# Exact search of a doubtful head rewrites its scores and threshold; one copy of the masking products

## The reference

```python
scores = jnp.einsum('bhqd,bhkd->bhqk', qn, kn)
temp = jax.nn.sigmoid(x.mean(axis=1) @ Wt + bt) + 0.5
scores = scores / temp[:, None, None, :]
kk = max(1, S // 4)
vals, idx = jax.lax.top_k(scores, kk)
w = jax.nn.softmax(vals, axis=-1)
rows = jnp.arange(B * H * S)[:, None]
attn = jnp.zeros((B * H * S, S), scores.dtype).at[rows, idx.reshape(-1, kk)].set(w.reshape(-1, kk)).reshape(B, H, S, S)
out = jnp.einsum('bhqk,bhkd->bhqd', attn, v)
```

## Time and profile before

| | us |
|---|---|
| median of three runs (3546.75 to 3565.47) | 3558.0 |
| the profiled execution | 3552.69 |
| its span, first to last instruction | 3550.8 |
| TensorE busy in it | 2939.5 |
| VectorE busy | 2754.0 |
| ScalarE busy | 2140.6 |
| GpSimd busy | 1797.6 |

### The profile page before, as it was taken

One profiled execution on the slowest core, in us unless ns is written; L12 is line 12 of the kernel. 1 busy time (PEld: TensorE's weight loads), 2 busy tenths in 40 slices (PEclk: granted clock), 3 DMA queues, 4 the chain that ended last, 5 costly groups with the idle time before them and its releaser, 6 DMA issues. The chain is left out here.

```text
span 3550.8 us, 59586 instructions
## 1 busy us (share of the span) xinstructions
PE 2939.5 (83%) x16154; PEld 1615.6 (45%) x16154; DVE 2754.0 (78%) x9472; ACT 2140.6 (60%) x5970; POOL 1797.6 (51%) x2285
## 2 busy tenths in 40 slices
PE   6798988878898689797887889788988889879755
PEld 3344444444454345454444445444544444444433
DVE  3787877878787787887878778787878888778872
ACT  2666666656666456665655667566665666566541
POOL 4355545545544455454554455465544556446533
PEclk9899999989998899999999999999989999899977
DMA  5000000000000000000000000000000000000000
GB/s 204 7 16 22 22 23 19 23 4 23 22 22 19 4 22 22 22 20 4 23 22 22 20 22 5 22 23 22 22 20 5 23 22 23 22 19 16 4 16 12
DMA packets 43575, 80.46 MB, mean 23 GB/s; under 512 B 3786, under 2 KB 11978, under 8 KB 43058
## 3 DMA queue, kind: packets, MB, share of 16 engines
q1 hardware_dynamic: 41554, 69.18, 5.8%
q0 software_dynamic: 1504, 5.77, 0.5%
HBM read 58.16 MB, written 16.78 MB: 21 GB/s over the span
## 5 line engine op out<-in xcount | busy, mean ns | idle before, releaser
L517 POOL TENSOR_SCALAR probs<-probs,kept_inv 128x256 f32<-128x256 f32 x1024 | 528.7, 536 | 892.1 <-DVE kept_inv L1769 892.1
L1730 DVE SCALAR_TENSOR_TENSOR probs<-scores,threshold,probs 128x256 f32<-128x256 f32 x1006 | 432.4, 493 | 206.9 <-issue 134.7
L1029 PE MATMUL work_ps<-ident,probs 128*128 128x128 f32 x2072 | 333.0, 297 | 182.9 <-POOL probs L517 123.6
L807 ACT ACTIVATE probsT<-work_ps 128x512 f32<-128x512 f32 x512 | 294.4, 596 | 303.8 <-PE work_ps L1029 287.9
L772 ACT ACTIVATE scores<-score_ps,neg_guess 128x256 f32<-128x256 f32 x1024 | 397.1, 483 | 103.7 <-DVE kept_inv L1769 98.1
L792 ACT ACTIVATE near<-scores 128x256 f32<-128x256 f32 x1024 | 412.8, 421 | 24.3 <-DVE nearest L1698 22.5
L1694 DVE MATCH_REPLACE8 near<-nearest,near 128x256 f32<-128x256 f32 x1024 | 406.9, 407 | 0.0
L1690 DVE MAX8 nearest<-near 128x8 f32<-128x256 f32 x1024 | 358.3, 411 | 6.3 <-DVE near L1682 4.7
L1029 PEld LDWEIGHTS work_ps<-ident,probs 128*128 128x128 f32 x2072 | 241.6, 149 | 263.2 <-POOL probs L517 120.2
L1698 DVE MAX8 nearest<-near 128x8 f32<-128x256 f32 x1024 | 356.9, 409 | 0.0
L484 POOL TENSOR_TENSOR inv_norm<-sumsq,minus_half 128x32 f32<-128x32 f32 x64 | 351.3, 5490 | 5.3
(11 more groups left out here) (171 smaller groups left out, 5535.4 us busy)
## 6 DMA issues: line engine op xcount, KB each, us to landing
x_in<-in_x_dram SPq DMA_DIRECT2D x32, 512.0 KB, 3.9
x_res<-in_x_dram SPq DMA_DIRECT2D x32, 512.0 KB, 4.6
out_dram<-rows SPq DMA_DIRECT2D x32, 512.0 KB, 3.1
c_sb<-in_ctx_dram SPq DMA_DIRECT2D x32, 256.0 KB, 2.7
scores<-in_L_ffn_W_dram SPq DMA_DIRECT2D x6, 1024.0 KB, 6.8
near<-in_L_ffn_W_dram SPq DMA_DIRECT2D x2, 1024.0 KB, 10.0
w_q<-in_L_attn_Wq_dram POOLq DMA_DIRECT2D x1, 1024.0 KB, 8.1
w_k<-in_L_attn_Wk_dram POOLq DMA_DIRECT2D x1, 1024.0 KB, 10.0
```

Source lines behind the costliest of these rows:

```text
L517: pool.tensor_scalar(probs[:, s % 2, h, j], probs[:, s % 2, h, j], kept_inv[:, s % 2, n:n + 1], 1.0, ALU.mult, ALU.mult).then_inc(s_pr, 1)
L807: act.activation(probsT[:, h, 2 * a:2 * a + 2], W[BANK_TP[s][2 * h + a]][:].rearrange("p (h k n) -> p h k n", h=2, k=NT), ACT.Copy).then_i ...
L1029: last = pe.transpose(dst[:, n * P:n * P + P], part, ident[:])
L1730: step.mark(dve.scalar_tensor_tensor(out=probs[:, r, h, j], in0=scores[:, r, h, j], scalar=threshold[:, r, k:k + 1], in1=probs[:, r, h, j] ...
```

## The change

A doubtful head's branch no longer ends in a product of its own. After the search, its scores are rewritten in place (1 where a score was struck out, else 0), its threshold is set to 0.5, and both are waited for. After the branches, eight `keep_above` stand once, and serve clean and doubtful units alike. The `Else` parts are gone, that of the unit and that of each head.

```diff
-                before = step.n
                 def keep_above(k):
                     h, j = divmod(k, HQ)
...
-                def keep_struck(k):
+                def take_out_struck(k):
 
                     h, j = divmod(k, HQ)
                     with dve.Fori(0, ROUNDS // 2):
                         strike(k)
                         strike(k)
                         slow.restart()
-                    step.mark(dve.scalar_tensor_tensor(
-                        out=probs[:, r, h, j], in0=scores[:, r, h, j], scalar=STRUCK / 2,
-                        in1=probs[:, r, h, j], op0=ALU.is_le, op1=ALU.mult, accum_out=kept_sum[:, r, k:k + 1]))
+                    slow.mark(dve.tensor_scalar(scores[:, r, h, j], scores[:, r, h, j], STRUCK / 2, None, ALU.is_le))
+                    slow.mark(dve.memset(threshold[:, r, k:k + 1], 0.5))
+                    slow.restart()
 
                 with dve.If(n > 0):
...
                     doubtful = dve.value_load(head_mask[0:1, 0:1], min_val=0, max_val=2 ** HS - 1)
                     for k in range(HS):
-                        step.n = before + k
                         with dve.If((doubtful & 2 ** k) > 0):
-                            keep_struck(k)
-                        with dve.Else():
-                            step.n = before + k
-                            keep_above(k)
-                with dve.Else():
-                    step.n = before
-                    for k in range(HS):
-                        keep_above(k)
+                            take_out_struck(k)
+                for k in range(HS):
+                    keep_above(k)
                 step.wait(step.n)
                 dve.reciprocal(kept_inv[:, r], kept_sum[:, r]).then_inc(s_inv, 1)
```

## The result

| | us |
|---|---|
| median after (6 runs, 3581.03 to 3590.4) | 3586.6 |
| median before beside it (6 runs, 3546.75 to 3566.47) | 3562.5 |
| ratio after / before, 95% interval | 1.0084 [1.0067, 1.0101] |
| the profiled execution after, its span | 3584.2, 3582.3 |

The change costs 0.84%, 24 us between the medians and 30 by the ratio. In a later comparison (e8) it cost 1.19% [1.0099, 1.0139]. Forecast was 3577: the sign was right and the time lies in the range, but the forecast stood on the edge of "no difference", and the result is clearly beyond it: the interval is 0.17% to either side. One of the 11 runs of the kernel before beside e5 to e8 took 5897.57 us, at a granted clock of 0.528, and is left out of every ratio.

What follows compares the result with a forecast made beforehand. VectorE's time from unit to unit was taken to bound the kernel. +50 us for doubtful units and -31 for freed stalls gave +19, so 3577 us against the median of 3558.0; own range 3562 to 3594, full range 3548 to 3610.

Steps and rivals of the forecast that it cites:

- What bounds the kernel: VectorE's time from unit to unit, up to `kept_inv`: time lost there reaches the total at a rate of 1 or little more.
- A struck head and the passes: Doubtful units: rewriting 0.6 us and seven bare passes of 0.34 make each 2.8 us longer, 17 of them 48 us.
- rival 1: Freed jump stalls outweigh a cheaper walk over the tests, so not slower: 3540 to 3560 us, chance 0.27.
- The stalls at the jump: Clean units' shorter jump over the search bodies frees 16 stalls of 2.26 us: 36 us, of which 31 is taken.
- the grid of 128: VectorE code comes in fixed blocks of 128 instructions; a jump landing in the next but one waits for a load.
- no stall in any clean unit: The block grid laid over the changed program gives no clean unit a stall behind its jump; 16 stalled before.
- A gain can end in a wait for another engine: Allowance on VectorE's freed stalls, since it already waits for ScalarE and GpSimd: -31 us taken where 36 was worked out.
- The sum: Whole kernel: +50 for doubtful units and -31 for freed stalls give +19 us on the profiled execution's 3552.7.
- under 0.5% can hardly be told from none: For the kernel's total time, a difference under 0.5%, 18 us, can hardly be told from none; the forecast lies on that edge.
- Rival 2: Clean units' jump stalls stay or move, so the -31 goes: 3608 us, 3639 at worst; chance 0.13.
- Rival 3: Search bodies stay eightfold in 24 places; undropped jumps to the next instruction would give 3582 us; counted with the forecast's chance.
- Rival 4: In each doubtful unit the bare walk over the tests waits for one code load, 17 x 1.5 us: 3603, chance 0.10.

Runs made afterwards that it cites:

- e8: The changed kernel run again unaltered, as reference and for a second profile; ratio 1.0119 to the kernel before.
- e5: The changed kernel with 28 one-column memsets ahead of VectorE's work, which shift its code; ratio 1.0225 to the kernel before.
- e2: The kernel before with 32 one-column memsets ahead of VectorE's work, which shift its code; ratio 1.0156 to the kernel before.
- e3: The changed kernel with 33 one-column memsets ahead of VectorE's work, which shift its code; ratio 1.0216 to the kernel before.
- e7: The changed kernel with a delay loop of eight memsets ahead of each doubtful unit's tests, code shifted by 45 memsets; ratio 1.0245 to the kernel before.
- e9: The changed kernel with 108 one-column memsets ahead of VectorE's work, which shift its code; ratio 1.009 to the kernel before.
- e1: The kernel before with 56 one-column memsets ahead of VectorE's work, which shift its code; ratio 1.0026 to the kernel before.
- e6: The kernel before with 59 one-column memsets ahead of VectorE's work, which shift its code; ratio 1.009 to the kernel before.

## Why the prediction was right or wrong, point by point

**What bounds the kernel** was right: what is added to VectorE between branch and `kept_inv` arrives in the time at a rate of about 1 (0.9 to 1.3 in e2, e3, e5 and e7; e7 against the changed kernel gave 0.8 to 1.1). The prediction had it from three turns that could not show it, since TensorE's clock was another in them (0.98, 0.92, 0.91): the value held, by luck in part.

**A struck head and the passes** (forecast 2.8 us a doubtful unit, bounds 1.8 and 3.6; the lower one adds up to 1.7). It is 2.26, near the point of 2.1 at which rival 1 would have won. The comparison with its `memset`, wait and clear was set at 0.6 us and a pass at 0.34; the first product came 2.33 us after the comparison's start, where 0.6 + 2.4 = 3.0 was foretold. The first test came 0.44 us behind the comparison's start and not 0.6, and a pass took 0.27. The step that was mis-sized is the pass of 0.34: in the row it was read from the earlier trace rows the engine's queue issues a clean head's product between each two tests (the first five of its products start at 3351.75, 3352.16, 3352.56, 3352.97 and 3353.38), so these were not bare passes. The term is 38 us and not 50.

**The stalls at the jump** (forecast 36 us freed, -31 taken). All 16 went, and the grid of 128 held for the full stalls of the shifted programs. The step of the prediction that failed is this -31, and in it "no stall in any clean unit": it asked whether the target's block was there, not whether the one behind it was. In the changed kernel the 5th and the 123rd unit wait 1.2 and 1.7 us (their branch stands a few instructions into a block), the fifth product of unit 3, even batch, 0.33, and an operation in unit 2 of the odd batch (L1682) 0.27 a turn: some 11 us in all.

**"A gain can end in a wait for another engine"** was the allowance, 5 us. The giving back was real, but of a kind I had not thought of: not a wait but a collision, 0.69 us in each of 13 units, 9 us. So of the 36 us some 16 remained, where 31 was forecast.

**The sum.** With the measured sizes it is +38 - 36 + 11 + 9 = +22 us on the profiled execution, and I had +19. That the two are so near is luck: 12 us too much for the doubtful units stood against 15 too much for the freed stalls. The profiled span grew by 31.5 (by 27.8 in e8). What the working lacked is the last 6 to 10 us in the profiles, and 8 to 20 in the ratios. The step from the sum to the verdict failed as well: "under 0.5% can hardly be told from none" had no row behind it, and with 6 runs on each side the interval is 0.17%, 6 us, to either side. Even the +19 of the forecast would have been told from none.

**The cause of the missing 6 to 20 us is open.** One candidate is TensorE's clock. For it: the lost clock, (1 - granted) x span, grew from 258 us (mean of 20 runs of the kernel before; 250 in the ten beside e8) to 282 and 289 (after, two comparisons); within the 23 runs of the kernel before next to e9, time and lost clock go together (correlation 0.88), 0.52 us of time for one of lost clock, so 24 to 39 us would make 12 to 20. Turns with the same work differ by 6 us with the clock. Against it: lost clock and time can have one cause, and no run here changed the clock alone. And e1 and e3 lost 13 and 18 us of clock against the kernel before beside them, while VectorE's local time explains all of the measured column; e6 lost 22, and there 14 us stay unexplained. Why the clock falls is plain only in part: a doubtful unit leaves TensorE without work longer, and e7, with the longest such gaps, had 0.913; but e1 and e6 lost clock too, with doubtful units as long as before. A run that keeps TensorE busy through the gap wasn't tried. A second candidate, waits of other engines that the collisions with L532 bring about, wasn't tested either: in e6 VectorE's wait before L1784 for GpSimd (L539) grew from 57.9 to 77.4 us, but with the change only to 59.1.

**The rivals.** Rival 1 (jumps win, not slower) is out, though the doubtful unit came close to its threshold. Rival 2 (stalls stay or move, 3608) was right in a small part: 11 of the 36 us came back as other waits. Rival 3 (one copy is not one): the order of instructions was as drawn. Rival 4 (the walk stalls too, one load waited for in each doubtful unit): 15 of the 17 doubtful units took 16.84 to 16.98 us, the one with two heads 26.80, and one 17.73; so a load is not waited for, but in the last perhaps.

**What would show it.** Right: issue before the products down by 32.7 (some 30 foretold), unit 1 starts 0.54 us behind its branch (726.2 and 726.72), and no other place waits a full 2.8. The sign of error "jumps stall in a new place" did come up, in the small waits above. Wrong: "passes show 0.34 us apart" (0.27); 17.4 us for the doubtful unit (16.93); the turn with three doubtful units 242 (238.9 from `kept_inv` to `kept_inv`, 235.3 before). The turn without doubtful units, from 199.1 to 197, was to decide, and it couldn't: the same turn lasted 203.6 after, at a clock of 0.95, and the four such turns 197.2 to 203.6.

## What to carry to other kernels

An idle that ends is not gained time until it is known what ran in it: look at the other engine in the stretch that closes up, above all at one that reads the same memory, and at what the next instruction needs. Code that is jumped over has a price that depends on where it stands against the grid of its loads; count the wait of the branch, of the landing and of the loop's jump back, and shift the code by some instructions to tell such a price from the edit's own. Branches cost nothing here as long as each had work queued over it (0.41 us from product to product with or without them); bare, they cost 1.9 us a doubtful unit, and grouping the tests took 0.56 of that back. Before adding up idle by what ended it, look whether a longer gap was only booked under another name.

## What the runs showed of the hardware that was not expected

- A VectorE product over 128x256 with two inputs and a GpSimd operation over 128x512 slow each other: 0.48 to 0.82 us for two of eight, and 1.52 to 2.25 us for GpSimd's pair.
- A wait for code can strike behind the landing of a jump: the second product (1.8 to 2.1 us), the third or fourth (1.1), the fifth (0.33, and 0.6 to 0.9 in e6), or an operation near the head of a loop's body (0.8, once a turn). Within the units the instruction that waited started 2.8 to 3.2 us behind the branch in every one of 82 cases.
- None of the three shifts tried on the kernel before made it faster (1.0026 with 56 `memset`s, 1.009 with 59, 1.0156 with 32). Two programs of this kernel that differ by a few dozen VectorE instructions early on differ in time by up to 1.6%.
- A passed test (register operation and taken branch) takes 0.27 us where seven stand bare, and 0.33 where a product is issued between two of them.
- The four turns of the same work in one execution lasted 197.2 to 203.6 us.
